# Moving a group's choice of expert ahead of the previous group's adapter, in one stage of a four-layer kernel

## The reference

```python
# end of _L1_xattn_ref
xt = x_text + y
h = layernorm(xt, g_ffn, b_ffn)
h = jax.nn.gelu(h @ W1 + b1, approximate=False) @ W2 + b2
xt = xt + h
return layernorm(xt, g_norm_out, b_norm_out)

# _L1_ffn_ref
base = jnp.einsum('btd,do->bto', x, W_base) + b_base
h = jax.nn.relu(jnp.einsum('btd,edh->ebth', x, Wd1) + bd1[:, None, None, :])
recon = jnp.einsum('ebth,ehd->ebtd', h, Wd2) + bd2[:, None, None, :]
losses = jnp.mean((recon - x[None]) ** 2, axis=(2, 3))
idx = jnp.argmin(losses, axis=0)
a = jax.nn.relu(jnp.einsum('btd,bdr->btr', x, Wa_down[idx]) + ba_down[idx][:, None, :])
adapter_out = jnp.einsum('btr,bro->bto', a, Wa_up[idx]) + ba_up[idx][:, None, :]
return base + adapter_out
```

## Time and profile before

| | us |
|---|---|
| median of 3 runs | 1450.48 |
| lowest, highest | 1449.17, 1454.42 |
| the profiled execution's own time | 1449.81 |
| its span (first to last instruction) | 1448.0 |
| PE busy | 1177.0 (81%) |
| DVE busy | 996.6 (69%) |
| ACT busy | 688.8 (48%) |
| POOL busy | 548.0 (38%) |
| mean granted TensorE clock | 0.869 of full speed |
| steps 3 to 7 of `stage_mix`, each | 17.16 |
| steps 8, 9, and what follows up to the next stage | 13.02, 13.37, 14.00 |

### The profile page before, as it was taken

One profiled execution on the slowest core, in us unless ns is written; L12 is line 12 of the kernel. 1 busy time (PEld: TensorE's weight loads), 2 busy tenths in 40 slices (PEclk: granted clock), 3 DMA queues, 4 the chain that ended last, 5 costly groups with the idle time before them and its releaser, 6 DMA issues. The chain is left out here.

```text
span 1448.0 us, 30742 instructions
## 1 busy us (share of the span) xinstructions
PE 1177.0 (81%) x10551; PEld 805.5 (56%) x10551; DVE 996.6 (69%) x3895; ACT 688.8 (48%) x2022; POOL 548.0 (38%) x770
## 2 busy tenths in 40 slices
PE   4767665667766579985899898599999989999998
PEld 3534323344534446653677677256666667776766
DVE  6767659999997379963577777677776654444443
ACT  3344245777675244421344444356666643333343
POOL 4576574777665255532222321333433220000000
PEclk8779875776675789996899999699999999898989
DMA  6400122000101411000000000000000000000000
GB/s 168 98 0 14 32 70 71 23 26 19 30 19 48 139 44 52 23 22 23 2 3 3 3 3 3 1 1 1 2 1 1 2 1 1 14 0 14 0 16 15
DMA packets 61249, 36.62 MB, mean 25 GB/s; under 512 B 19477, under 2 KB 58992, under 8 KB 61106
## 3 DMA queue, kind: packets, MB, share of 16 engines
q1 hardware_dynamic: 59802, 34.48, 8.4%
q10 hardware_dynamic: 1304, 0.33, 0.1%
HBM read 25.21 MB, written 6.42 MB: 22 GB/s over the span
## 5 line engine op out<-in xcount | busy, mean ns | idle before, releaser
L2988 DVE SCALAR_TENSOR_TENSOR k_X<-ps,m_gt,k_X 128x128 f32 (+1 forms) x256 | 72.2, 344 | 120.2 <-PE ps L2872 120.0
L2911 ACT ACTIVATE m_hid<-ps,k_b 128x512 f32<-128x512 f32 x128 | 81.5, 684 | 132.8 <-PE ps L2872 127.0
L2872 PEld LDWEIGHTS ps<-k_w,m_hid 128*128 128x128 f32 x1024 | 123.1, 192 | 26.8 <-issue 19.4
L2861 PE MATMUL ps<-m_xnT,k_w 128*128 128x512 f32 x256 | 127.5, 628 | 1.3 <-PEq L72 1.3
L2872 PE MATMUL ps<-k_w,m_hid 128*128 128x128 f32 x1024 | 123.4, 275 | 0.0
L2532 POOL TENSOR_TENSOR l_p<-l_p,l_rsum 128x512 f32<-128x512 f32 x64 | 65.2, 1039 | 139.1 <-DVE l_rsum L2810 139.1
L2345 DVE TENSOR_REDUCE g_top<-ps 128x8 f32<-128x1024 f32 x64 | 75.4, 1219 | 50.6 <-PE ps L2213 50.6
L2293 ACT ACTIVATE g_pT<-ps 128x1024 f32<-128x1024 f32 x64 | 62.0, 1021 | 84.8 <-PE ps L2229 84.8
L2664 ACT ACTIVATE l_p<-ps,l_shift 128x128 f32<-128x128 f32 x256 | 91.4, 389 | 21.1 <-DVE l_shift L2751 19.9
L1587 DVE MATCH_REPLACE8 v_left<-c_top,v_left 128x128 f32<-128x128 f32 x384 | 100.8, 275 | 0.0
L711 PE MATMUL ps<-f_expT,f_xeT 128*128 128x512 f32 x128 | 73.8, 709 | 27.4 <-DVE k_X L1089 27.3
(11 more groups left out here) (538 smaller groups left out, 3131.5 us busy)
## 6 DMA issues: line engine op xcount, KB each, us to landing
v_toep<-kpad SPq DMA_DIRECT2D x4, 1024.0 KB, 9.2
fo_dram<-c_fo SPq DMA_DIRECT2D x32, 128.0 KB, 1.7
d_fo<-fo_dram SPq DMA_DIRECT2D x8, 512.0 KB, 3.6
d_mine<-d_wad SPq DMA_DIRECT2D x32, 96.5 KB, 1.9
k_X<-in_x SPq DMA_DIRECT2D x8, 256.0 KB, 3.5
v_late<-kpad SPq DMA_DIRECT2D x2, 1024.0 KB, 8.1
out<-k_X SPq DMA_DIRECT2D x8, 256.0 KB, 2.4
f_cx<-in_ctx SPq DMA_DIRECT2D x4, 384.0 KB, 5.6
```

The lines of the kernel that those rows point to most:

```text
L2861: pe.matmul(ps[:, 4 * u + q, :], k.w1_3[:, e, 128 * q:128 * q + 128], xnT[:, u], start=True, stop=True).then_inc(s["hid_ps"].sem, 1)
L2872: m = pe.matmul(ps[:, 4 * u + 2 + e % 2, j * S:j * S + S], hid[:, u, q, j * S:j * S + S], k.w2_3[:, e, q, :], start=q == 0, stop=q == 1)
L2911: act.activation(hid[:, u, q, :], ps[:, 4 * u + q, :], ACT.Gelu, bias=k.b1_3[:, 2 * e + q:2 * e + q + 1]).then_inc(s["hid"].sem, 1)
L2988: dve.scalar_tensor_tensor(out=xj[u][j], in0=ps[:, 4 * u + 2 + e % 2, j * S:j * S + S], scalar=gt[:, u, j, e:e + 1], in1=xj[u][j], op0=ALU ...
```

## The change

On PE the MLP's second product of group n and `sums` of group n-2 come before down and up of group n-3. On DVE the choice of group n-2 comes before xo of group n-3. Because the choice of the next group may now be written while SP could still be reading the last one, `at` has two buffers.

```diff
-        gain, best, at = tmp("gain", [G, 8]), tmp("best", [G, 8]), tmp("at", [G, 8], U32)
+        gain, best, at = tmp("gain", [G, 8]), tmp("best", [G, 8]), tmp("at", [G, 2, 8], U32)
@@ SP
-                    chosen = [sp.value_load(at[j:j + 1, 0:1], min_val=0, max_val=E - 1) for j in range(G)]
+                    chosen = [sp.value_load(at[j:j + 1, a, 0:1], min_val=0, max_val=E - 1) for j in range(G)]
@@ PE
+            def sums(g):
+                pe.wait_ge(sx_done, g + 1)
+                pe.wait_ge(loss_done, g + 1)
+                o = ps[0:G, 5, 0:8]
+                pe.matmul(o, loss[:, 0, :], k.indic[:, 0, :], start=True, stop=False)
+                pe.matmul(o, loss[:, 1, :], k.indic[:, 1, :], start=False, stop=False)
+                pe.matmul(o, sx[:], k.bd2T[:], start=False, stop=False)
+                pe.matmul(o, k.ones[:, 0:G], k.bd2q[:], start=False, stop=True).then_inc(sum_ps, 1)
@@ PE, in the loop, after recon(n - 2, 1)
+                if has(n):
+                    if n >= 1:
+                        pe.wait_ge(left, n)
+                    pe.wait_ge(hid_done, 4 * (n + 1))
+                    for j in range(G):
+                        for q in range(4):
+                            m = pe.matmul(ps[:, 7, j * S:j * S + S], hid[:, q, j * S:j * S + S], k.w2_1[:, q, :],
+                                          start=q == 0, stop=q == 3)
+                    m.then_inc(mlp_ps, 1)
+                if has(n - 2):
+
+                    sums(n - 2)
                 if has(n - 3):
                     g = n - 3
                     if has(n):
...
                     m.then_inc(dn_ps, 1)
-                if has(n):
...
                 if has(n - 3):
                     g = n - 3
...
                     m.then_inc(out_ps, 1)
-                if has(n - 2):
...
@@ DVE
+            def choose(g):
+                dve.wait_ge(sum_ps, g + 1)
+                dve.tensor_scalar(gain[:], ps[0:G, 5, 0:8], -1.0, None, ALU.mult).then_inc(gain_done, 1)
+                dve.wait_ge(gain_done, g + 1)
+                dve.max(best[:], gain[:]).then_inc(best_done, 1)
+                dve.wait_ge(best_done, g + 1)
+                dve.max_index(at[:, g % 2, :], best[:], gain[:]).then_inc(at_done, 1)
@@ DVE, in the loop, after z
+                if has(n - 2):
+                    choose(n - 2)
                 if has(n - 3):
                     g = n - 3
                     xg = group(k.X, g)
                     dve.wait_ge(out_ps, g + 1)
...
-                if has(n - 2):
...
```

## The result

The changed kernel takes 1461.61 us (median of 4, 1459.71 to 1462.85) where the kernel before takes 1449.99 (median of 4): ratio 1.0073, 95% interval 1.0049 to 1.0097. Forecast were 1457.5 us and a range of 1451 to 1464. The profiled execution has a span of 1457.9 us against 1448.0. Ratios leave out single executions in a slow state, and differ a little from the quotients of the medians.

What follows compares the result with a forecast made beforehand. PE and DVE were both taken as full in steps 3 to 6 (16.73 and 16.51 of 17.16 us). Terms 5.28 + 0.37 + 2.71 - 1.37 = +7.0 us on 1450.48 gave 1457.5 us, range 1451 to 1464.

Steps and rivals of the forecast that it cites:

- Rival 2: Clock dips in steps 3 to 6, 3.1 us each: one gives 1460.6, one in each 1469.9; chance 0.17.
- The ring of the full steps: Steps 3 to 6: DVE statistics through loss, sums, down, xo to DVE again, 18.48 us against 17.16; +1.32 each, +5.28.
- The MLP's earlier end buys nothing: Full steps: the MLP ends 1 us earlier without gain, as DVE comes late to z by its own queue.
- The second buffer, SP's part: Two buffers of `at`, read by SP with the same 4 loads a group: cost 0.
- Step 7: DVE has no next group's z to make, so sums does not wait; the step lasts 17.53 us: +0.37.
- Step 8: No MLP left; down and up, formerly hidden, start behind the wait for loss: 14.71 us against 12.00, +2.71.
- Step 9: The last choice no longer stands behind xo and starts 0.65 us after loss instead of 2.02: -1.37.
- The clock: Half-clock dips around the last steps' idle stretches: taken as 0, a dip moving from step 9 to 8; bounds +1.3, -4.4.
- Rivals 1, 3 and 4: Wait for loss hidden, 1453.7, chance 0.13; last hand-over makes it faster, 1447.8, 0.05; order moves nothing, 1450.5, 0.05.
- Rival 3: Last hand-over decides: -1.37, and -1.3 from the clock, 1447.8; without step 9's dip 1444.7; chance 0.05.

Runs made afterwards that it cites:

- second set: The unmodified changed kernel run once more for a second profile, against the kernel before: 1459.83 us, ratio 1.0070.
- the MLP first, alone: Kernel before with only the MLP's second product moved ahead of down on PE, sums and the choice staying last: 1453.11 us against 1449.51.
- step 8 back in the old order: Changed kernel with step 8 alone put back in the old order on PE and DVE: 1455.65 us.
- the filling of steps 8 to 10 alone: Changed kernel with products that nothing reads put into PE's idle stretches of steps 8, 9 and 10: 1454.11 us.
- `loss` earlier: Changed kernel with DVE's order altered: sq and loss before the addition to X and statistics, then z, choice, xa, xo: 1456.35 us.

## Why the forecast was right, point by point

The median of 1461.61 lies within the range, but above the forecast's own 1454.5 to 1460: the loss is 11.6 us by the medians (9.9 in the second set) and 9.9 by the first profile's span, where +7.0 was forecast. The waits were foreseen rightly, the clock was not. Rival 2 with one dip, 1460.6, lies nearer to the median, but by accident: its dip was there in one profile of two and cost 1.2 us, not 3.1.

- **The ring of the full steps** (+1.32 each, +5.28): shown. 18.38 to 18.51 us a step in both profiles of the changed kernel, but for the one step with a dip; the wait 1.03 to 1.07 in steps 4 to 6, xo waiting 1.75 there, and filling PE's gap changed nothing. Its parts are shown apart: the relu in the open 0.36 a step (the MLP first, alone), the wait for `loss` the rest. The ring gave the wait as 0.95; the row says 1.04, because PE leads the statistics by 0.87 us (605.18 to 606.05) and not by 0.78.
- **The MLP's earlier end buys nothing**: right. DVE reaches z (602.43 in step 5) with no wait before it.
- **The second buffer, SP's part**: right, 6.37 us from choice to down as before.
- **Step 7** (+0.37): +0.61 in the first profile, in which step 6's dip reaches into it, +0.20 in the second.
- **Step 8** (+2.71): the mechanism was right. Measured +5.00, of which down to xo at half clock is 5.87 - 3.47 = 2.4; with the clock held up by fillers the step is 2.64 longer than before (645.65 to 660.29). The idle stretch was forecast as 5.1 us and is 5.25.
- **Step 9** (-1.37): the choice starts 0.53 (672.47 - 671.94) behind `loss`, 0.65 forecast; -1.82 and -1.34 in the two profiles. Part of this is the clock: step 9's PE work takes 13.93 and 14.23 us.
- **The clock**: this is the term that was mis-sized. The sum took it as 0, "a dip that moves"; it measured +3.0 us in the second profile (2.3 in step 8, 1.04 in step 10, the rest of the terms 0.3 below) and +4.2 in the first, with step 6's 1.2. The dips did not move from step 9 to step 8: they became longer. The changed kernel's steps 8 and 9 show 0.79 and 0.70, and step 10 0.50, where before step 8 stood at 1.00, one stretch of 6.8 us at 0.53 lay in step 9, and step 10 was up again for its last products. The bound I gave, +1.3, was taken from that step 10, partly at full clock, though the work of step 8 can fall at half clock as a whole. Both the term and its upper bound were too low; that the sum stayed within the range is owed to the range's width.
- **Rival 2** (dips in the full steps), the rule of the Trainium skill ("TensorE: Matmul & The Clock Gate", section "A second HAM failure mode: psum-queue depth-cycling"): in one of two profiles a dip stood at the end of step 6, at 1.2 us; of the two variants with the same full steps and the same gaps (step 8 back in the old order, and the filling of steps 8 to 10 alone) neither had it. The gap of 1 us a step can go with a dip, but does not bring one each time, and why that one came is open. A granted clock under 1.00 within steps 3 to 7 was named as a sign of being wrong, so this sign came, once.
- **Rivals 1, 3 and 4** fell with the first row of the ring. Rival 3's price was real (the last hand-over gives -1.4), but alone all but 0.4 of it is taken back by the clock.

## What to carry to other kernels

Before putting an operation with a late input early in an engine's order, lay the ring through both engines: what stands behind it waits, too, and the step grows by the ring, not by the wait. In the tail of a pipeline, where nothing covers, ask of each idle stretch of TensorE whether the products after it then run at half clock, and price that beside the stretch itself: here 5.25 us of idle time cost another 2.4. A gain of a microsecond there may need idle time filled before it shows.

## What the runs showed that I had not expected

- After 5.25 us without a product, all of down and up ran at half clock: 5.87 us for 3.47. In the same place fillers of 4.45 us kept 1.00, with 0.97 us left idle. No more than 1.2 us of idle time before `sums` in step 8 also went with a dip at once behind it, in the kernel before.
- Starting work earlier after an idle stretch may win nothing: the last down began 1.35 us earlier and xo 0.3 us earlier (only step 9 changed).
- The same code ahead of the stage ends at different times: the first `loss` ended between 547.14 and 552.03 us in the profiles. Differences of 2 us between two executions say little here; the time cut within the stage says more.
- DVE's four instructions that make xa took 1.98 us together instead of 1.11 when they stood later in the step (`loss` earlier); why is open.
